# Loading cross-attention's inputs during self-attention, into the tile in which the weights of self-attention were staged

## What is computed

```python
x = x + self_attention(layernorm(x))                       # 16 heads of 64, 100 keys
x = x + cross_attention(layernorm(x), ctx_1024, mask, ...) # 16 heads of 16, 361 keys of ctx (32, 361, 256)
x = x + moe_ffn(layernorm(x))                              # 8 experts, each token goes to its argmax expert
```

```python
q = split_heads(decoder_hidden @ Wq.T + bq)
k = split_heads(encoder_hidden @ Wk.T + bk)
v = split_heads(encoder_hidden @ Wv.T + bv)
scores = jnp.where(encoder_mask == 0, -inf, q @ k.T * scale)
out = softmax(scores) @ v @ Wo.T + bo
```

## Time and profile before

| what | value |
|---|---|
| time, median of 3 runs | 1718.27 us (1717.52 to 1718.36) |
| time of the profiled execution | 1719.54 us |
| its span, first to last instruction | 1717.6 us |
| mean granted TensorE clock | 0.946 of full speed |
| busy: PE, weight loads of PE, DVE, ACT, POOL | 88%, 76%, 62%, 44%, 25% |

### The profile page before, as it was taken

The page is one execution under the profiler, slowest core; times in us unless marked ns, Lnnn a source line. Parts: engine busy times, 40 slices in busy tenths (PEclk is TensorE's granted clock), DMA queues, the critical chain, the costliest instruction groups (busy, mean ns, idle before and its releaser), DMA issues. The chain is left out here.

```text
span 1717.6 us, 39303 instructions
## 1 busy us (share of the span) xinstructions
PE 1512.1 (88%) x12244; PEld 1299.5 (76%) x12244; DVE 1057.3 (62%) x2627; ACT 763.3 (44%) x1830; POOL 426.4 (25%) x564
## 2 busy tenths in 40 slices
PE   4799999999999999829999999999996309999997
PEld 3687878787878787727888888888885307888886
DVE  5658585858585857426777777677773305555553
ACT  3536363646464646314555555655652002222221
POOL 4112121212121211142222222222212153333332
PEclk9999999999999999868999999999997558999999
DMA  5703030303030303057667667677651243555551
GB/s 181 194 1 78 1 76 0 76 0 76 0 76 0 76 0 77 1 131 202 179 184 199 184 183 197 181 192 191 180 135 51 53 134 116 180 184 178 180 179 50
DMA packets 159949, 195.71 MB, mean 114 GB/s; under 512 B 83724, under 2 KB 128307, under 8 KB 159636
## 3 DMA queue, kind: packets, MB, share of 16 engines
q1 hardware_dynamic: 154356, 186.09, 39.7%
q0 software_dynamic: 3968, 6.59, 1.2%
q10 hardware_dynamic: 1568, 2.30, 0.4%
HBM read 138.63 MB, written 58.05 MB: 115 GB/s over the span
## 5 line engine op out<-in xcount | busy, mean ns | idle before, releaser
L1198 DVE TENSOR_REDUCE row_max<-psb_s 100x1 f32<-100x361 f32 x512 | 263.5, 531 | 143.5 <-PE psb_s L1341 137.5
L1090 ACT ACTIVATE probs<-psb_t 121x400 f32<-121x400 f32 (+1 forms) x384 | 190.4, 507 | 114.2 <-PE psb_t L1351 111.7
L419 POOL TENSOR_TENSOR diag<-neg_ident,row_max 100x400 fp32r<-100x400 f32 x128 | 112.2, 898 | 375.1 <-PE ps_t L666 203.6
L1341 PE MATMUL psb_s<-k,q 97*100 97x362 f32 x512 | 186.2, 367 | 15.4 <-DVE row_max L1198 8.3
L1351 PE MATMUL psb_t<-q,k 98*121 98x200 f32 (+1 forms) x768 | 147.4, 274 | 2.6 <-ACT probs L1090 2.0
L2021 PE MATMUL psd_h<-h_in,w_sb 128*128 128x256 f32 x640 | 143.8, 383 | 1.4 <-ACT h_in L1887 1.4
L2029 PE MATMUL psd_y<-w_sb,hid 128*128 128x256 f32 x640 | 144.5, 379 | 0.0
L2021 PEld LDWEIGHTS psd_h<-h_in,w_sb 128*128 128x128 f32 x640 | 123.2, 193 | 19.0 <-issue 1.8
L2029 PEld LDWEIGHTS psd_y<-w_sb,hid 128*128 128x128 f32 x640 | 120.1, 190 | 15.5
L1351 PEld LDWEIGHTS psb_t<-q,k 98*121 98x121 f32 (+1 forms) x768 | 125.5, 184 | 7.6 <-ACT probs L1090 5.1
L376 ACT CAST o_hi<-ps_ot 64x200 fp32r<-64x200 f32 x256 | 82.1, 321 | 100.1 <-PE ps_ot L691 95.2
(11 more groups left out here) (225 smaller groups left out, 3674.7 us busy)
## 6 DMA issues: line engine op xcount, KB each, us to landing
w_sb<-in_w SPq DMA_DIRECT2D x40, 1024.0 KB, 7.8
packed_keys<-k_st SPq DMA_DIRECT2D x32, 724.0 KB, 3.7
k<-packed_keys SPq DMA_DIRECT2D x64, 362.0 KB
v_rows<-v_tok SPq DMA_DIRECT2D x32, 400.0 KB
v_ext<-v_rows SPq DMA_DIRECT2D x32, 400.0 KB
q<-packed_queries SPq DMA_DIRECT2D x64, 200.0 KB
k<-packed_keys SPq DMA_DIRECT2D x64, 181.0 KB
c_t<-in_contextT SPq DMA_DIRECT2D x32, 361.0 KB, 4.6
```

The lines of the kernel that those rows point to most:

```text
L419: pool.tensor_tensor(diag[:, g % 2], c.neg_ident[0:S, 0:S].unsqueeze(1).to_broadcast([S, GH, S]), row_max[:, g // 2 % 2, g % 2].unsqueeze( ...
L1090: act.activation(probs[0:KT[kt], u % 2, kt], ps_t[i % 2][0:KT[kt], 0:4 * S], ACT.Exp, scale=HD2 ** -0.5).then_inc(probs_ready, 1)
L1198: dve.reduce_max(row_max[:, p, h:h + 1], ps_s[h % 2][0:S, 0:S2], AX_X).then_inc(max_ready, 1)
L1341: pe.matmul(ps_s[h % 2][0:S, 0:S2E], q2[0:97, p, u, g, S * a:S * (a + 1)], k2[0:97, p, u, g], start=True, stop=True).then_inc(scores_ready, 1)
```

## The change

What was `w_stage` is now `c.stage`, allocated for the whole program. `stage_for_cross_attention` cuts it into the weights, biases, masks and the first context of cross-attention. SP issues their transfers in self-attention, after the values of quad 0, together with the clearing of `packed_queries` and a store of ones to a new DRAM tensor `ones_rows`. POOL clears the mask tiles after its weight splits and makes bias and masks before the last quad; SP stores the bias after the last quad. Cross-attention loses these steps. Its packed rows of ones now come from two transfers of one row each (3200 and 5792 words), and PE waits for them only before the first scores. Waits at its start are fewer, and the first steps of POOL, DVE and PE change places.

```diff
+def stage_for_cross_attention(c, ctx, nc):
+    at = [0]
+    def take(words):
+        at[0] += words
+        return c.stage[:, at[0] - words:at[0]]
...
+    c.first_context = take(KD * S2).rearrange("p (k s) -> p k s", k=KD)
@@ self_attention, sync
+            def cross_inputs():
+                sp.wait_ge(vo_lo_ready, 2)
+                for dst, src in ((c.wk_st, cross["wk"]), (c.wv_st, cross["wv"]), (c.wq_sb, cross["wq"]),
+                                 (c.wo_sb, cross["wo"])):
+                    sp.dma_start(dst, src.rearrange("(k p) n -> p k n", p=128)).then_inc(c.cross["w2_loaded"], 16)
...
+                sp.dma_start(c.first_context, cross["ctxT"][0].rearrange("(k p) s -> p k s", p=128)
+                             ).then_inc(c.cross["ctx_loaded"], 16)
...
+                sp.dma_start(cross["ones"], c.ones_f[:]).then_inc(c.cross["ones_stored"], 16)
+                sp.wait_ge(c.cross["mask_cleared"], 2)
...
+            values_through(0)
+            cross_inputs()
+            with sp.Fori(1, QUADS) as q:
+                values_through(q)
+            sp.wait_ge(c.cross["bias_ready"], 1)
+            sp.dma_start(cross["kb"], c.bias_b.bitcast(F32)).then_inc(c.cross["bias_stored"], 16)
+            sp.wait_ge(c.cross["bias_stored"], 16)
+            sp.wait_ge(c.cross["ones_stored"], 16)
+            sp.wait_ge(c.cross["q_cleared"], 16)
@@ self_attention, gpsimd
+            pool.wait_ge(vo_lo_ready, 2)
+            pool.memset(c.mask_t, 0).then_inc(c.cross["mask_cleared"], 1)
+            pool.memset(c.mask_b, 1).then_inc(c.cross["mask_cleared"], 1)
...
             with pool.Fori(0, QUADS - 1) as q:
                 quad(q, False)
+            cross_masks()
             quad(QUADS - 1, True)
@@ cross_attention, sync
-            context(0, 0)
             context(1, 1)
...
+            sp.dma_start(q2[96:97].rearrange("p b u g s -> p (b u g s)").bitcast(F32),
+                         ones(16 * 2 * S)).then_inc(ones_placed, 16)
+            sp.dma_start(k2[97:98].rearrange("p b u g n -> p (b u g n)").bitcast(F32),
+                         ones(16 * S2E)).then_inc(ones_placed, 16)
@@ cross_attention, gpsimd
+            split_context(0, 0)
             inverse_root(0)
-            split_context(0, 0)
+            split_context(1, 1)
             inverse_root(1)
-            split_context(1, 1)
+            pool.memset(v_ext[:, :, :, :, HD2:32], 0.0).then_inc(pad_ready, 1)
+            pool.wait_ge(pad_ready, 3)
             live(0, 0)
@@ cross_attention, vector
-            dve.wait_ge(w_lo_ready, 2)
             norm_stats(0)
+            low_bits(0, wk_hi, wk_lo, wk_st)
+            low_bits(1, wv_hi, wv_lo, wv_st)
+            keys(0, 0, 0)
             normalize(0)
             norm_stats(1)
             normalize(1)
             norm_stats(2)
-            keys(0, 0, 0)
             queries(0, 0)
@@ cross_attention, tensor
             pe.wait_ge(w_loaded, 16 * 8)
-            pe.wait_ge(w_hi_ready, 2)
-            pe.wait_ge(w_lo_ready, 2)
-            pe.wait_ge(pad_ready, 5)
+            pe.wait_ge(w_lo_ready, 1)
+            pe.wait_ge(pad_ready, 2)
...
+            keys(-2, 0, 0)
             turn_x(-3, 1)
-            keys(-2, 0, 0)
             queries(-2, 0)
...
+            pe.wait_ge(w_lo_ready, 2)
             values(-1, 1, 0)
+            pe.wait_ge(ones_placed, 32)
             for h in range(9):
                 scores(0, 0, h)
```

More of the change, by code:

```diff
@@ L109, in at_batch, with weight, self_attention @@
     return tensor[:, bass.ds(b, 1), cols].rearrange("p b d -> p (b d)")
-def self_attention(nc, c, x, wqkT, wvT, woT, v_dram, xs):
+def stage_for_cross_attention(c, ctx, nc):
[3 more added lines that the diff above has]
+        return c.stage[:, at[0] - words:at[0]]
+    def weight():
+        return take(KD * D).rearrange("p (k n) -> p k n", k=KD)
+    c.wk_st, c.wv_st, c.wq_sb, c.wo_sb = weight(), weight(), weight(), weight()
+    c.bq_sb, c.bk_sb, c.bv_sb = take(KD), take(KD), take(KD)
+    c.bo_sb = take(D)[0:S]
+    c.mask_t, c.key_dead, c.key_live = (take(3 * B)[0:KT[0]].rearrange("p (k b) -> p k b", k=3) for _ in range(3))
+    c.mask_t = c.mask_t.bitcast(I32)
+    c.mask_b = take(S2E)[0:B].bitcast(I32)
+    c.bias_b = take(S2E)[0:B].bitcast(F32R)
+    c.first_context = take(KD * S2).rearrange("p (k s) -> p k s", k=KD)
+    for name in ("w2_loaded", "mask_cleared", "mask_t_loaded", "mask_b_loaded", "key_mask_ready", "bias_ready",
+                 "bias_stored", "ctx_loaded", "q_cleared", "ones_stored"):
+        c.cross[name] = ctx.enter_context(nc.semaphore(name + "_x"))
+def self_attention(nc, c, x, wqkT, wvT, woT, v_dram, xs, cross):
     with ExitStack() as ctx:
@@ L780, in cross_attention @@
         pool_passed = sem("pool_passed")
-        w_loaded = sem("w2_loaded")
+        w_loaded = c.cross["w2_loaded"]
         w_hi_ready = sem("w2_hi_ready")
         w_lo_ready = sem("w2_lo_ready")
[L784 to L789, removed]
+        ones_placed = sem("ones_placed")
         pad_ready = sem("pad_ready")
-        ctx_loaded = [sem(f"ctx_loaded{p}") for p in range(2)]
+        ctx_loaded = [c.cross["ctx_loaded"], sem("ctx_loaded1")]
         c_hi_ready = sem("c_hi_ready")
@@ L880, in _, with ones @@
         def _(sp):
[L881 to L886, removed]
+            def ones(n):
+                return ones_dram.rearrange("r n -> (r n)")[0:n].rearrange("(o n) -> o n", o=1)
             def context(b, p):
@@ L2063, in build @@
         qd = nc.dram_tensor("packed_queries", (2, 2, 128, KD, 2 * S), F32, kind="Internal").ap()
-        cross_attention(nc, c, ins["contextT"], ins["mask"], ins["maskT"], kb_dram, kd, qd, ins["wq2T"], ins["wk2T"], ins["wv2T"],
-                        ins["wo2T"], ins["bq"], ins["bk"], ins["bv"], ins["bo"])
+        ones_dram = nc.dram_tensor("ones_rows", (128, 128), F32, kind="Internal").ap()
+        c.stage = sb("stage", [128, 2 * KD * O1])
+        c.cross = {}
+        stage_for_cross_attention(c, ctx, nc)
+        cross = {"ctxT": ins["contextT"], "mask": ins["mask"], "maskT": ins["maskT"], "wq": ins["wq2T"],
+                 "wk": ins["wk2T"], "wv": ins["wv2T"], "wo": ins["wo2T"], "bq": ins["bq"], "bk": ins["bk"],
+                 "bv": ins["bv"], "bo": ins["bo"], "qd": qd, "kb": kb_dram, "ones": ones_dram}
+        self_attention(nc, c, ins["x"], ins["wqkT"], ins["wvT"], ins["woT"], v_dram, xs, cross)
+        cross_attention(nc, c, ins["contextT"], kb_dram, kd, qd, ones_dram)
         with ExitStack() as late:
```

105 lines of the change are left out of this document (43 added, 62 removed).

## The result

The changed kernel takes 1701.59 us (median of 4 runs, 1700.51 to 1702.25), the kernel before beside it 1718.32 us (4 runs, 1717.52 to 1718.98). The ratio is 0.9902, with a 95% interval of 0.9885 to 0.9919: 16.7 us less. The profiled execution took 1702.25 us and spans 1700.3, at a mean clock of 0.948.

A forecast was written before the change was run, and what follows sets the result against it. The prediction took a serial start-up, an idle hole at the start of cross-attention, to bound the kernel. A 19.3 us advance, of which 15.4 were left, plus 1.3 from the clock gave 1701.6 us from 1718.27, range 1698.0 to 1707.0.

The forecast's parts named there:

- What bounds the kernel: Start of cross-attention: an idle hole made by a serial start-up; what it loses, the program gains one for one.
- The context: Start of cross-attention: with loads and masks gone, PE's first keys start at 734.6 instead of 753.92, 19.3 us earlier.
- a meeting on SBUF: DVE's weight splits and POOL's context split exclude each other on SBUF ports; cost 0.7 us, bounds 0 and 1.4.
- Keys before `xn`: First batch: DVE normalizes only after the keys, so context and `xn` come one after the other; 3.2 us lost.
- The second context: SP's first transfer in cross-attention, split by POOL ahead of batch 1's root; cost 0, at worst 1 us.
- the first rival: Second context lands late, or DVE and POOL meet on SBUF several times, delaying the queries; 1703 to 1708 us, chance 0.10.
- The rows of ones: Two one-row transfers replace POOL's clearings; needed only at the first scores, 20 us later, so hidden.
- PE's clock: Scores, keys and queries of batch 0 run at full clock sooner; gain 1.3 us, bounds -1 and +2.
- What moves into self-attention: 16 transfers behind quad 0's values, and POOL's mask work and clearings, fit in idle time; cost 0.
- the second rival: Transfers in quad 0 not hidden, value rows up to 5 us late; 1702 to 1707 us, chance 0.06.
- the fourth: Slower: moved transfers and waits block SP's queue, delaying quad 1's values; 1733 us if they last until 170, chance 0.015.
- The sum: Whole kernel: -15.4 - 1.3 = -16.7 us, from the median of 1718.27 to 1701.6 us.

The follow-up runs named there:

- before_again: The kernel before, unchanged and run once more to see the spread of a profiled execution; 1719.03 us.
- warm: The changed kernel plus 44 transposes of the identity, results unread, filling PE's idle time at the start of cross-attention; 1702.82 us, ratio 0.9898.
- late_warm: The kernel late plus transposes of the identity, results unread, in PE's idle time at the start of cross-attention; 1697.65 us, ratio 0.9881.
- after_again: The changed kernel, unchanged and run once more on another chip; 1703.84 us, ratio 0.9918.
- loads_back: The changed kernel with the weights, biases and first context loaded at the start of cross-attention again; 1712.24 us.
- masks_back: The changed kernel with the masks' clearing, loading and arithmetic and the bias store back at the start of cross-attention; 1710.33 us.
- ones_by_pool: The changed kernel with the rows of ones filled by POOL again, ahead of the context's split, instead of by two transfers; 1709.99 us.
- late: The changed kernel with batch 0's root inside the first context's split, batch 2's root ahead of the second context, `wv_lo` after the keys; 1701.72 us, ratio 0.9900.

## Why the prediction was right

The predicted time, 1701.6 us, was met by 1701.59. By its own steps, that is better than its terms deserve: the main term held, and that the total came out within 0.1 us is luck.

- **What bounds the kernel**: right. The start-up is one serial chain, and the three kernels with a part put back show that a us ahead of the first `c_lo` is a us of the block.
- **The context**: I expected the first keys 2.8 us behind the start without a meeting on SBUF and 3.5 with it; they are at 3.08. The term was 0.4 us too dear. The engine that stands is mostly not the one I chose: DVE's `wk_lo` went ahead and held `c_lo` for 0.33 us, and then `c_lo` held `wv_lo`, 2.06 us instead of 0.69, which cost nothing.
- **Keys before `xn`**: expected 3.2 us lost, measured 3.7: from the start of the keys to the end of `q_st` it takes 8.57 us where it took 4.85. I had 8.1. The excess is in the last step: PE's queries take 2.00 us where they took 1.68, and DVE begins its `q_st` at 741.85, though ACT's is done at 741.57, because batch 1's `xn` took 1.44 us instead of some 0.4. The clock was 0.50 all through these queries, while before it came back to 1.00 at 757.2, within them. This error and the one above cancel, and the end of `q_st`, forecast at 11.6 us, is at 11.65.
- **The second context**: landed at 735.2, POOL waited 0.23 us for it. Cost 0, as said; a late landing, the first rival's main case, is out. Its other case, several meetings on SBUF, came in small: batch 1's `xn` beside the clearing is some 0.3 of the excess above. **The rows of ones**: no wait for them. From `q_st` to the first scores 11.38 us, expected 11.6.
- **PE's clock**: this term failed. I had taken a gain of 1.3 us in the steps that answer to the earlier trace rows. Three rows of PE after the change:

```profile
753.75 0.54 PE L1370 MATMUL psb_s<-k,q 97*100 97x362 f32 x2 [2.31 <-DMA k<-packed_keys]
...
766.90 0.57 PE L1380 MATMUL psb_t<-q,k 98*121 98x200 f32 x2
...
771.31 0.39 PE L1370 MATMUL psb_s<-k,q 97*100 97x362 f32 x1
```

  The same steps take 4.41 us, where they took 4.33 before and 3.07 in batch 1. The clock is 0.92 at 750 to 755 us, 0.50 from 755 to 770, and 0.88 up to 775. The reason I gave, that PE's bursts stand closer together, was not enough: PE still stands still ahead of the first scores. The 4.33 it was reckoned from does not repeat either: before_again, the same program, takes 3.69. Over the profiles without transposes these steps take 3.7 to 4.5 us, in the three with them 2.8 to 3.6. The prediction also said that the clock's return is not in the program's hands; with the transposes it is back at 1.00, and stays there until the thin end, from 21.9 us behind the block's start in warm and from 15.4 in late_warm, where the changed kernel has it from 40.5.
- **What moves into self-attention**: 0, as said; the second rival and the fourth are out. Rows of SP, PE and POOL in self-attention after the change, in three fences:

```profile
86.27 0.32 SPq L355 DMA_DIRECT2D stage<-in_mask  x1
137.78 3.09 SPq L328 DMA_DIRECT2D v_rows<-v_tok  x2
```

```profile
88.03 0.84 PE L713 MATMUL ps_o<-v_ext,probs 100*100 100x65 f32 x8
```

```profile
624.04 1.46 POOL L476 TENSOR_SCALAR stage<-stage 32x362 fp32r<-32x362 int32 x1
625.58 0.47 POOL L479 TENSOR_SCALAR stage<-stage 121x96 f32<-121x96 int32 x1
626.13 0.45 POOL L481 TENSOR_SCALAR stage<-stage 121x96 f32<-121x96 f32 x1
670.42 2.38 POOL L491 TENSOR_TENSOR diag<-neg_ident,row_max 100x400 fp32r<-100x400 f32 x2 [43.85 <-DVE row_max L583]
```

  SP has issued the last mask at 86.6 us (15 transfers and not 16; the bias follows after the last quad) and next has work at 137.78; batch 2 of quad 0 is weighted at 88.03, no later than before (88.89); POOL's mask work still leaves 43.85 us of idle time.
- **The sum**: 15.3 of the 15.4 us came. In place of the clock's 1.3 the profile has 1.2 us in small differences along the block and 1.08 in front of it, of which the latter is spread. The total agreed because the missing term was about as large as the spread of a single profile; after_again, at 1703.84 us and 0.9918, stands 14.9 us below its own before by the medians and 14.1 by the ratio, nearer to the 15.4 without the clock term than to 16.7. The two ratios' intervals overlap.

## What to carry to other kernels

When a block opens with a long wait, list everything that stands ahead of its first useful step, and move all of it: here three causes of 7 to 9 us each lay side by side, and any one left behind would have kept half of the hole. Behind the last one the order of small steps decides, and it is read from the end (here `q_st`, on which the transfers hang): an order that starts PE earlier, as this one does, gives nothing if the last input comes later for it. A gain that rests on the granted clock should not be counted on while PE's gaps stay: in none of the profiles without the transposes did the expected 1.3 us come in full.

## What was not expected of the hardware

A clearing on POOL, which only writes, held DVE. `xn` (TENSOR_SCALAR, 100x256) takes 0.40 to 0.42 us alone and 1.44 us beside the MEMSET of `v_ext`, from 739.71 to 741.15, where the clearing ends at 741.00. The same 1.44 us stand in after_again and in warm, loads_back, masks_back and ones_by_pool, and where late starts the clearing later, `xn` takes 0.40. A TENSOR_TENSOR of DVE is not held by a clearing: in ones_by_pool `wk_lo` took 0.66 us, at 732.12, inside the 2.76 us of `q`'s, and 0.69 in the kernel before. Beside POOL's `c_lo`, which reads, both stand: `wv_lo` 2.06 us, `xn` 1.66. The Trainium skill has it so (page "SBUF — State Buffer", section "Who interferes with whom"): a `tensor_scalar` of VectorE in a mode that uses both port pairs shuts out any GpSimd operation and is shut out by it, while one with two SBUF inputs meets only those that read. The rows agree with each case, as far as they go: none names the mode in which `xn` ran. The prediction had weighed meetings with the context's split alone, and none with a clearing.

The second is how much the clock at 1.2 GHz costs at the two ends of the block, away from the steady part: 2.3 us in the start-up (36.18 against 33.92), and some 5 at the thin end of cross-attention, in one of fourteen profiles.
